# Moving a Hadamard transform from the FFN weights to the activations, and doing without a preparation stage

## The reference, cut to what matters

```python
def fwht(x): ...                       # normalised Walsh-Hadamard transform over the last axis
x = fwht(x * SU_ug) / 64               # 512 wide
x_up   = x @ W_up.T   * (Wscale_ug[:2048] * 64)
x_gate = x @ W_gate.T * (Wscale_ug[2048:] * 64)
x = silu(x_gate) * x_up                # 2048 wide
x = fwht(x * SU_dp) / 64
x = x @ W_down.T * (Wscale_dp * 64)    # back to 512
```

## Time and profile before

| | us |
|---|---|
| median of 3 runs | 1794.69 (1794.46 to 1931.85) |
| the profiled execution, its span | 1794.5 |
| PE busy | 1643.7 (92%), 7952 matmuls |
| DVE busy | 956.4 (53%) |
| ACT busy | 679.4 (38%) |
| POOL busy | 290.2 (16%) |
| mean granted PE clock | 0.966 of full speed |

### The profile page before, as it was taken

One profiled execution on the slowest core, in us unless ns is written; L12 is line 12 of the kernel. 1 busy time (PEld: TensorE's weight loads), 2 busy tenths in 40 slices (PEclk: granted clock), 3 DMA queues, 4 the chain that ended last, 5 costly groups with the idle time before them and its releaser, 6 DMA issues.

```text
span 1794.5 us, 23492 instructions
## 1 busy us (share of the span) xinstructions
PE 1643.7 (92%) x7952; PEld 1353.6 (75%) x7952; DVE 956.4 (53%) x1615; ACT 679.4 (38%) x1323; POOL 290.2 (16%) x423
## 2 busy tenths in 40 slices
PE   5989988898898565799999999999999999999997
PEld 3967777687687454588888888888888888888886
DVE  6665766667576379534543534544534444534444
ACT  3144235225225343333433433434434434434433
POOL 4142243124124189100000000000000000000000
PEclk8999999999998877999999999999999999999999
DMA  6040021012102270100010100100100100100100
GB/s 228 1 148 15 29 86 74 32 54 94 42 19 82 70 238 36 47 0 0 25 47 0 47 24 0 70 0 0 70 0 23 47 0 23 47 0 0 47 0 24
DMA packets 35479, 80.21 MB, mean 45 GB/s; under 512 B 3008, under 2 KB 3408, under 8 KB 34128
## 3 DMA queue, kind: packets, MB, share of 16 engines
q1 hardware_dynamic: 34512, 75.08, 12.1%
q10 hardware_dynamic: 576, 2.10, 0.3%
q0 software_dynamic: 320, 2.11, 0.3%
HBM read 54.11 MB, written 25.17 MB: 44 GB/s over the span
## 4 chain that ended last, share of the span: by engine, by line
PE 58%; DVE 0%; ACT 0%; issue 0%; POOL 0%; POOLq 0%; DVEq 0%; ACTq 0%
PE ff_g_ps L85 7%; PE ff_g_ps L86 7%; PE ff_g_ps L87 7%; PE ff_acc L85 6%; PE ff_acc L87 6%; PE ff_acc L86 6%; PE ff_u_ps L85 6%; PE ff_u_ps L86 6%; PE ff_u_ps L87 6%; DVE ff_bn L1507 0%; DVE ff_y L1505 0%; ACT ff_x_hi L1366 0%; DVE ff_gu_lo L1443 0%; ACT ff_y L1427 0%; DVE ff_mv L1510 0%
## 5 line engine op out<-in xcount | busy, mean ns | idle before, releaser
L1442 DVE TENSOR_TENSOR ff_gu_lo<-w_wg,ff_gu_hi 128x512 fp32r<-128x512 f32 x128 | 88.7, 693 | 482.8 <-ACT ff_gu_hi L1372 482.7
L1386 ACT ACTIVATE ff_h_hi<-ff_hf 128x512 fp32r<-128x512 f32 x128 | 80.9, 632 | 345.7 <-DVE ff_hf L1452 345.7
L85 PE MATMUL ff_g_ps<-ff_x_hi,ff_gu_hi 128*128 128x512 f32 x512 | 200.4, 391 | 7.5 <-DVE ff_gu_lo L1443 7.5
L1379 ACT ACTIVATE ff_sg<-ff_g_ps,w_ug_scale 128x512 f32<-128x512 f32 x128 | 88.1, 688 | 297.7 <-PE ff_g_ps L87 297.7
L86 PE MATMUL ff_g_ps<-ff_x_lo,ff_gu_hi 128*128 128x512 f32 x512 | 200.1, 391 | 0.0
L87 PE MATMUL ff_g_ps<-ff_x_hi,ff_gu_lo 128*128 128x512 f32 x512 | 199.9, 390 | 0.0
L86 PE MATMUL ff_u_ps<-ff_x_lo,ff_gu_hi 128*128 128x512 f32 x512 | 199.2, 389 | 0.0
L85 PE MATMUL ff_u_ps<-ff_x_hi,ff_gu_hi 128*128 128x512 f32 x512 | 199.2, 389 | 0.0
L85 PE MATMUL ff_acc<-ff_d_hi,ff_h_hi 128*128 128x512 f32 x512 | 199.2, 389 | 0.0
L86 PE MATMUL ff_acc<-ff_d_lo,ff_h_hi 128*128 128x512 f32 x512 | 199.2, 389 | 0.0
L87 PE MATMUL ff_u_ps<-ff_x_hi,ff_gu_lo 128*128 128x512 f32 x512 | 199.2, 389 | 0.0
(11 more groups left out here) (249 smaller groups left out, 3328.7 us busy)
## 6 DMA issues: line engine op xcount, KB each, us to landing
at_xt<-in_xt SPq DMA_DIRECT2D x4, 2048.0 KB, 9.1
at_xn<-in_x SPq DMA_DIRECT2D x32, 256.0 KB, 3.0
x_scratch<-at_x SPq DMA_DIRECT2D x32, 256.0 KB, 2.1
x1t_scratch<-at_x1t SPq DMA_DIRECT2D x32, 256.0 KB, 3.2
w_xraw<-x1t_scratch SPq DMA_DIRECT2D x8, 1024.0 KB, 5.6
ff_y<-x_scratch SPq DMA_DIRECT2D x8, 1024.0 KB, 5.6
out<-ff_y SPq DMA_DIRECT2D x7, 1024.0 KB, 4.2
wp_stage<-in_wg SPq DMA_DIRECT2D x4, 1024.0 KB, 8.6
```

The source lines that it names most:

```text
L85: pe.matmul(out, lhs_hi, rhs_hi, start=first, stop=False)
L1379: act.activation(sg[q][:, :], g_ps[:, :], ACT.Silu, scale=ug_scale[:, 1, bass.ds(i, 1)]).then_inc(silu_s.sem, 1)
L1386: act.activation(h_hi[q][:, :], hf[q][:, :], ACT.Copy).then_inc(h_hi_s.sem, 1)
L1442: dve.tensor_tensor(gu_lo[q][:, 0, :, :], gate_up_chunk(wg, i), gu_hi[q][:, 0, :, :].bitcast(F32), ALU.subtract)
```

## The change: what it does, and the diff

- The preparation block is gone. Gate and up weights are loaded as they are, straight into the FFN's SBUF tensors.
- The 512-wide transform is done on x1. In the FFN, block k transposes the x1 of block k+1 chunk by chunk (128 of the 512 columns): PE turns four 128x128 tiles into one PSUM bank at steps 5, 7, 9 and 11; ACT and DVE split them into `xs_hi`/`xs_lo` with the signs `su` at the end of the same steps; PE multiplies by the sign matrix at steps 6, 8, 10 and 12 into the same bank; ACT copies the result to `xm`; POOL's `butterfly` does the 4-wide part with eight operations of 128x512; at step 14 ACT and DVE split the result into `x_hi`/`x_lo`. For the first block all this happens ahead of the first gate matmul, in four PSUM banks.
- `y` is double, since it is now needed two blocks at a time: it is loaded a block earlier, and the transposes read it.
- The down weight's 16-wide part is done by POOL in attention (`mix_down`): two pieces of 128x1024 a batch, four stages of two operations each, loaded and stored by SP. Its 128-wide part is done in the first FFN block, one full float32 matmul per step and DVE's `fold_down` for the output scale. `sd` goes into the scale of the up product.
- Attention no longer transposes, copies and stores x1 a second time. Its wkv, wqs and scale loads are issued by ACT instead of POOL.
- The FFN's inner loop over steps is written out; the loop over pairs of blocks stays.

```diff
@@ attention, SP
-                def store_transposed(t):
-                    sp.wait_ge(*x1t_s.now(b, t + 1))
-                    sp.dma_start(x1t_dram[b, t], x1t[:, t % 2, :]).then_inc(x1t_out[t % 2].sem, 16)
+                def load_down(k):
+                    if k == 0:
+                        sp.wait_ge(wo_lo_s, 8)
+                    sp.wait_ge(*(wd_out.now(b, 16) if k else wd_out.last(b, 32)))
+                    sp.dma_start(wd_a[:, :, :], io["wd"][b * 2 + k]).then_inc(wd_in.sem, 16)
+                def store_down(k):
+                    sp.wait_ge(*wd_mixed.now(b, 8 * k + 8))
+                    sp.dma_start(mixed_dram[b * 2 + k], wd_a[:, :, :]).then_inc(wd_out.sem, 16)
...
+                    if t == 0:
+                        store_down(0)
+                    if t == 1:
+                        load_down(1)
+                    if t == RT:
+                        store_down(1)
@@ attention, POOL
-            pool.dma_start(scales[:, :], io["logit_scale"]).then_inc(ls_in, 16)
-            pool.dma_start(wkv[:, :, :], io["wkv"]).then_inc(wkv_in, 16)
-            pool.dma_start(wqs[:, :, :], io["wqs"]).then_inc(wqs_in, 16)
+            def mix_down(b, k, stage):
+                src, dst = (wd_a, wd_b) if stage % 2 == 0 else (wd_b, wd_a)
+                pair = lambda t: t[:, :, :].rearrange("p (h two l) n -> p h two (l n)", two=2, l=1 << stage)
...
+                pool.tensor_tensor(pair(dst)[:, :, 0], pair(src)[:, :, 0], pair(src)[:, :, 1], ALU.add).then_inc(wd_mixed.sem, 1)
+                pool.tensor_tensor(pair(dst)[:, :, 1], pair(src)[:, :, 0], pair(src)[:, :, 1], ALU.subtract).then_inc(wd_mixed.sem, 1)
             with pool.Fori(0, B) as b:
                 split_x(b, 0)
                 split_x(b, 1)
+                mix_down(b, 0, 0)
+                mix_down(b, 0, 1)
                 split_x(b, 2)
+                mix_down(b, 0, 2)
+                mix_down(b, 0, 3)
                 split_x(b, 3)
                 for t in range(RT):
                     inverse_deviation(b, t)
...
+                    if t in (2, 3):
+                        mix_down(b, 1, t - 2)
...
                         normalise(b, tt, p)
+                        if tt == 0 and p in (3, 5):
+                            mix_down(b, 1, 2 + p // 5)
@@ attention, ACT
+            act.dma_start(scales[:, :], io["logit_scale"]).then_inc(ls_in, 16)
+            act.dma_start(wkv[:, :, :], io["wkv"]).then_inc(wkv_in, 16)
             for c in range(DC):
                 act.dma_start(wq_raw[c], io["wq"][:, c, :]).then_inc(wq_in[c], 16)
+            act.dma_start(wqs[:, :, :], io["wqs"]).then_inc(wqs_in, 16)
@@ FFN, SP: the order of the first transfers
+            fetch(0, 0, 0)
+            for t, n in ((ident, "ident"), (had, "had"), (su, "su"), (sd, "sd"), (dps, "dps"), (ug_scale, "ug_scale")):
+                sp.dma_start(t[:], io[n]).then_inc(tab_in, 16)
+            weights(0)
+            down_weights(0)
+            weights(1)
+            fetch(1, 0, 1)
+            weights(2)
+            down_weights(1)
+            weights(3)
+            def body(blk, idx, parity, first, last):
                 if not first:
+                    sp.wait_ge(*normed.last(blk, 1))
+                    sp.dma_start(out_dram[blk - 1], y[1 - parity][:, :, :]).then_inc(stored.sem, 16)
+                    if not last:
+                        sp.wait_ge(*stored.last(blk, 16))
+                        fetch(blk + 1, idx + parity, 1 - parity)
@@ FFN, POOL
+            def butterfly(blk, first):
+                m = lambda k: xm[:, k, :]
+                pool.wait_ge(*xm_s.now(blk, 2))
...
+                pool.tensor_tensor(m(4), m(0), m(1), ALU.add).then_inc(mixed.sem, 1)
+                pool.tensor_tensor(m(5), m(0), m(1), ALU.subtract).then_inc(mixed.sem, 1)
+                pool.wait_ge(*xm_s.now(blk, 4))
...
@@ FFN, ACT
+            def split_turned(blk, c, bank):
+                act.wait_ge(*xt_ps.now(blk, c + 1))
+                act.wait_ge(*(xh_ps.now(blk, c) if c else xh_ps.last(blk, DC)))
+                act.activation(xs_hi[:, :], bank, ACT.Copy, scale=su[:, c:c + 1]).then_inc(xs_hi_s.sem, 1)
+            def keep_mixed(blk, c, bank):
+                act.wait_ge(*xh_ps.now(blk, c + 1))
...
+                act.activation(xm[:, c, :], bank, ACT.Copy).then_inc(xm_s.sem, 1)
...
+                for i in range(1, IC):
+                    s, q = blk * IC + i, i % 2
+                    chunk_work(s, i, q, first)
...
                     round_h(s, q)
...
+                    if not last:
+                        for c in range(DC):
+                            if i == BEGIN + 2 * c:
+                                split_turned(blk + 1, c, x_ps[:, :])
+                            if i == BEGIN + 2 * c + 1:
+                                keep_mixed(blk + 1, c, x_ps[:, :])
+                        if i == IC - 2:
+                            for c in range(DC):
+                                split_x(blk + 1, c, 1 - parity)
...
+            for c in range(DC):
+                split_turned(0, c, acc[:, c, :])
+                if c == 0:
+                    split_gu(0, 0, 0, True)
+                keep_mixed(0, c, acc[:, c, :])
@@ FFN, DVE
+            def split_turned(blk, c, bank):
+                dve.wait_ge(*xs_hi_s.now(blk, c + 1))
+                dve.scalar_tensor_tensor(xs_lo[:, :], bank, su[:, c:c + 1], xs_hi[:, :].bitcast(F32), ALU.mult, ALU.subtract).then_inc(xs_lo_s.sem, 1)
+            def fold_down(i):
+                dve.wait_ge(w_had, i + 1)
+                dve.tensor_tensor(down_chunk(i), by_piece(w_ps), by_piece(dps), ALU.mult).then_inc(w_fold, 1)
...
+                    if first:
+                        fold_down(i)
+                    if not (last and i == IC - 1):
+                        split_gu(s + 1, (i + 1) % IC, 1 - q)
+                    chunk_work(s, i, q)
                     lower_h(s, q)
...
+                            if i == BEGIN + 2 * c:
+                                split_turned(blk + 1, c, x_ps[:, :])
@@ FFN, PE
+            def turn_x(blk, idx, c, parity, bank, free):
+                if c == 0:
+                    pe.wait_ge(*x1_in[parity].now(idx, 16))
+                if free:
+                    pe.wait_ge(*(xm_s.now(blk, c) if c else xm_s.last(blk, DC)))
+                for t in range(FT):
+                    i = pe.transpose(bank[:, P * t:P * t + P], y[parity][:, t, P * c:P * c + P], ident[:, :])
+                i.then_inc(xt_ps.sem, 1)
+            def mix_x(blk, c, bank):
+                pe.wait_ge(*xs_lo_s.now(blk, c + 1))
+                pe.matmul(bank, hr[:, :], xs_hi[:, :], start=True, stop=False)
+                pe.matmul(bank, hr[:, :], xs_lo[:, :], start=False, stop=True).then_inc(xh_ps.sem, 1)
+            def mix_down(i):
+                pe.wait_ge(wd_in[i // 8], 16)
+                if i:
+                    pe.wait_ge(w_fold, i)
+                pe.matmul(w_ps[:, :], had[:, :], down_chunk(i), start=True, stop=True).then_inc(w_had, 1)
...
+                for i in range(1, IC):
+                    s, q = blk * IC + i, i % 2
+                    if first:
+                        mix_down(i)
+                    if not last:
+                        for c in range(DC):
+                            if i == BEGIN + 2 * c:
+                                turn_x(blk + 1, idx + parity, c, 1 - parity, x_ps[:, :], True)
+                            if i == BEGIN + 2 * c + 1:
+                                mix_x(blk + 1, c, x_ps[:, :])
                     gate_up(s, q, parity)
...
```

More of the change, by code:

```diff
@@ L49 @@
 FT = FB // P
+WC = 64
+WP = D // WC
 class Signal:
@@ L880, in local_keys @@
             def local_keys(b):
-                pe.wait_ge(*x1t_s.last(b, TILES - 1))
                 for t in range(LT):
@@ L1252, in ffn_block @@
         h_lo = [sb(f"h_lo{i}", [P, FB], F32R) for i in range(2)]
-        y = sb("y", [P, FT, D])
+        y = [sb(f"y{i}", [P, FT, D]) for i in range(2)]
         bn, mv, power = sb("bn", [P, FT, 6]), sb("mv", [P, FT, 2]), sb("power", [P, 3, FT])
@@ L1474, in statistics @@
                     dve.bn_aggr(mv[:, t, :], bn[:, t, :]).then_inc(bn_s.sem, 1)
-            def body(blk, parity, first, last):
-                def step(i, q, wrap):
-                    s = blk * IC + i
-                    if wrap and last:
-                        return
-                    nxt = 0 if isinstance(i, int) and i == IC - 1 else (1 if wrap else i + 1)
-                    if not (last and isinstance(i, int) and i == IC - 1):
-                        split_gu(s + 1, nxt, 1 - q)
-                    chunk_work(s, 0 if wrap else i, q)
-                    lower_h(s, q)
-                    if wrap:
-                        residual(blk)
-                    if isinstance(i, int) and i == 1 and not first:
-                        statistics(blk - 1)
-                    if isinstance(i, int) and i == IC - 2 and not last:
```

(71 more changed lines are left out.)

443 lines of the change are left out of this document (149 added, 294 removed).

## The result

The changed kernel takes 1817.84 us (median of 4 runs, 1815.37 to 1819.28) against 1794.6 for the one before: a ratio of 1.013, 95% interval 1.0117 to 1.0142. It is slower by 1.3%, inside the two per cent that count as no change. The forecast was 1810, range 1778 to 1840. The profiled execution has a span of 1815.0.

What follows compares the result with a forecast made beforehand. PE bounds the FFN blocks without slack; in attention waits matter too. From 1794.5: -83.8 startup, +92.6 blocks, +2 POOL, +6.6 folds, +4 turns, -7 attention, +1 loads = 1809.9; forecast 1810 us, 8-in-10 range 1778 to 1840.

Steps and rivals of the forecast that it cites:

- mixing step over 8.16: FFN steps 6, 8, 10, 12: PE waits 1.68 us for DVE's low half, plus 0.45 of matmuls and 0.08.
- later turning step over 8.16: FFN transposes after a block's first four: PE waits 0.80 us for ACT to empty the PSUM bank, plus 0.44 and 0.08.
- POOL beside DVE, a block: Step 13 of FFN blocks: POOL's butterfly operations hold DVE's low halves, 0.3 us of stall a block, +2 in all.
- 15 folds: First FFN block: fifteen float32 128x512 matmuls folding the down weight, 0.44 us each on PE, +6.6.
- loop turns: FFN's two-block loop, unrolled inside: instruction fetch after the taken branch costs 2 us on each of two turns, +4.
- main step: All FFN blocks but the last: transposes, mixing and PE's waits for DVE and ACT cost 13.2 us each, +92.6.
- The startup: Before the first gate matmul: preparation goes, the new startup takes 34.2 us from the first transfer; gate matmul 83.8 earlier.
- Attention: Attention without x1's second transposes: most waits move to the chain behind; 1.8 us a batch gained, -7 in all.
- the stalls did happen: Rival in the FFN: ACT and DVE finish before the step's end, no stalls, 1742 us; chance 0.08.
- the clock stayed at 1.00: Rival in the FFN: PE's clock falls, each of 28 mixing stalls costs 1.7 us more, 1858 us; chance 0.08.
- POOL's folding is free: Attention: POOL's folding taken as costing 0; the rival had it hold DVE, +25 us, 1835; chance 0.08.
- the -31 of attention: Rival: attention gives back all the work it loses, -31 us instead of -7, 1786 us; chance 0.06.

Runs made afterwards that it cites:

- both_late: Changed kernel with PE's transposes and mixing matmuls both moved behind the step's gate/up matmuls; 1750.5 us, ratio 0.976 to the kernel before.
- after_nofold: Changed kernel without the float32 matmuls of the down weights for chunks 1 to 15 and their scaling; 1813.5 us, ratio 1.0116 to the kernel before.
- late_nofold: both_late without the float32 matmuls of the down weights for chunks 1 to 15 and their scaling; 1740.6 us, ratio 0.970 to the kernel before.
- fold_f32r: both_late with each down-weight fold as two fp32r matmuls, behind the gate/up matmuls of the step before; 1747.1 us, ratio 0.974 to the kernel before.

## Why the prediction was right, step by step

Measured values are those of the profiled execution.

| step | predicted | measured |
|---|---|---|
| first FFN transfer | 613.0 (619.0 - 7 + 1) | 618.59; 612.7 to 618.9 in nine profiles |
| from it to the first gate matmul | 34.2 | 33.9; 33.9 to 36.0 in nine profiles |
| from there to the first Silu | as before | +1.1 |
| transposes, four at a time | 0.44 | 0.47 |
| mixing step over 8.16 | 2.21 (1.68 + 0.45 + 0.08) | 2.30 |
| later turning step over 8.16 | 1.32 (0.80 + 0.44 + 0.08) | 1.33 |
| POOL beside DVE, a block | 0.3 | 0.35 |
| 15 folds | 6.6, all in the open | 5.7: 0.89 each, eight inside waits |
| loop turns | 4 | 0.1 |

- **The main step held**: the stalls were read from the order of operations on DVE and ACT behind the product, with no trace of them to look at, and came within 5%: 13.2 us a block against 13.7. The two experiments that took one stall away show the mechanism, and both together took PE's waits to none.
- **The startup held** to 0.3 us in sum in the profiled execution, and to 0.9 in the mean of nine. Two of its parts were high and cancelled lower ones: the tables were in use 7.1 us after the first transfer instead of 10, the first weights after 12.5 instead of 14; then a chunk took 3.27 instead of 3.0, and POOL's operations 1.26 to 1.6 instead of 1.2.
- **The folds came out right for two wrong reasons.** The row of 7.03 us for "x16" was read as sixteen full matmuls; it is eight, each shown as two instructions. So a fold costs 0.89. The page "FP8 and Floating Point Precision" of the Trainium skill, section "TensorE Precision Notes", says true FP32 takes four passes through the array; the trace agrees, 4 x 0.2267 = 0.91 beside 0.89. And "all in the open" failed too: eight of the fifteen stand ahead of a matmul that would have waited anyway. A size half of the true one, times about twice the number that is paid, gave 6.6 by luck. In both_late, with seven of those waits gone, the same folds cost twice as much.
- **Attention** was predicted 6 us shorter beside the 1.8 for the store that went. The profiled execution shows 2.2 in all instead of 7.8, the mean of nine 5.3. The argument (waits move to the chain behind) is what the waits show. The size in the one profile is off by a spread of 6 us between executions that a single trace of before does not reveal.
- **The loop turns** failed: no block start in the changed kernel is over 0.1 us longer than before. Where the loop turns (blocks 3 and 5) other kernels show up to 1.3 (after_nofold, block 5) and 1.1 (late_nofold, block 3), still under the 2 a turn that the sum has.
- **Missed**: the table load. A fixed cost was hidden in the preparation; with its cover gone it is on the path, 1.28.
- The rivals: the stalls did happen (28 and 18 times, and block 0's three at the transposes were filled by the folds); the clock stayed at 1.00 in the changed kernel's blocks; POOL's folding is free; the -31 of attention did not come. POOL and DVE do meet: DVE's low halves of the gate and up weights took 1.42 and 1.78 instead of 0.69 and 0.68 (929.80 and 931.14), of which the 1.7 of slack took most; 0.35 a block was left, and nothing once the mixing was moved. The page "SBUF — State Buffer" of the Trainium skill, section "SBUF: two separate sides", has a lock for a whole instruction; the trace agrees: DVE's operation of 929.80, 0.69 long alone, ends 0.55 after POOL's has ended (930.67), and POOL's next, 1.26 long alone, 1.15 after DVE's (931.22).

The sum was too high by 4 (turns) and 1.2 (folds and startup), too low by 5.6 (first transfer), 1.1 (first Silu) and 3.5 (stalls and POOL): 1809.9 + 5.0 = 1814.9, of 1815.0. So errors of 5 and of 10 us partly cancelled; the stalls, 64 of the 92.6 us set down for the blocks, are the part that was known. (Two slips in the recorded working are 0.1 each: 15.7 + 3 x 3.0 put as 24.6, and 7 x 13.24 as 92.6.)

## What to carry to other kernels

When extra work goes into the queue of an engine without slack, its own length is the small part: here it was 3.7 us a block (4 x 0.47 + 4 x 0.455), and its waits 10.0 (4 x 1.85 + 3 x 0.87). Ask for each added instruction when its last input is made, counted from the event that paces the other engines, and put it behind that event; the same matmuls, standing 5.4 us further down the queue, turned 1.3% slower into 2.4% faster. And price work that shares a queue with a stall twice, once with the stall and once without: part of it is hidden now, and comes due when the stall is mended.

## What the runs showed of the hardware

- A float32 matmul of 128x512 holds TensorE for 0.89 us at full clock, an fp32r one for 0.2267; in the rows it is two instructions, so "x16" there is eight matmuls.
- PE idle for 2.2 us in attention, where it is not full before and after, was followed by 17 us at 1.2 GHz; 28 stalls of 1.85 us between full steps of 8 us left it at 2.4 GHz.
- At the head of block 0's second step, some 10 us behind the first gate matmul, a wait of 2.3 us (late_nofold) and one of 1.8 (fold_f32r) were followed by 3 us and more at 1.2 GHz, which cost 1.6; one of 2.1 (after_nofold) and eight of 1.3 to 1.4 (other traces, with the float32 fold in front) were not. What decides stays open.
- 37 us (at full clock) of filling transposes in attention changed the time by nothing that could be measured, and raised its mean clock from 0.92 to 0.96.
- A 1 MB piece of the weights landed 14.9 us after its issue, with eighteen transfers issued one behind another at the startup, against 8.6 in the preparation, whose loads waited for their buffers.
